# Two projections around a relative attention, each as one written-out block, with one product for both key biases

## The reference, cut to what matters

```python
x = x + rel_attention(layernorm(x), ...)     # q, k, v = h @ W.T + b
#   logits = q k + q rk,  rk[q, k] = embK[clip(k - q, -64, 64) + 64];  w = softmax(logits)
#   out = w v + w rv,     rv from embV in the same way;                out @ Wo.T + bo
x = x + ffn(layernorm(x), ...)
#   h = layernorm(x) * ln1_g + ln1_b;  q, k, v = split(h @ w_qkv + b_qkv);  attention;  @ w_o + b_o
#   then a second layernorm, a top-2 gate over 8 experts, and the experts
```

## Time and profile before

| | us |
|---|---|
| median of 3 runs | 4641.74 |
| lowest and highest | 4637.56, 4656.35 |
| profiled execution | 4656.61 |
| its span in the profile | 4654.9 |
| PE busy | 4083.6 (88%) |
| VectorE busy | 3683.7 (79%) |
| ScalarE busy | 2998.9 (64%) |
| GpSimd busy | 1451.0 (31%) |

### The profile page before, as it was taken

The page is one execution under the profiler, slowest core; times in us unless marked ns, Lnnn a source line. Parts: engine busy times, 40 slices in busy tenths (PEclk is TensorE's granted clock), DMA queues, the critical chain, the costliest instruction groups (busy, mean ns, idle before and its releaser), DMA issues. The chain is left out here.

```text
span 4654.9 us, 79857 instructions
## 1 busy us (share of the span) xinstructions
PE 4083.6 (88%) x26893; PEld 2141.6 (46%) x26893; DVE 3683.7 (79%) x6653; ACT 2998.9 (64%) x5840; POOL 1451.0 (31%) x1418
## 2 busy tenths in 40 slices
PE   2869999999999999997566999999999997769997
PEld 1424444444444444443332333333333332669997
DVE  2678888888888888885467888888888897557775
ACT  0207777777777777775122888888888886246664
POOL 0025666666665656664100000000000000523232
PEclk9959999999999999998785999999999999779999
DMA  2746666666666666665545323323323322676664
GB/s 88 252 99 154 159 164 164 160 166 159 162 168 144 171 148 168 155 165 128 179 162 107 48 40 45 48 40 46 48 39 46 48 39 38 172 213 174 174 178 113
DMA packets 507780, 578.05 MB, mean 124 GB/s; under 512 B 67316, under 2 KB 447268, under 8 KB 497340
## 3 DMA queue, kind: packets, MB, share of 16 engines
q1 hardware_dynamic: 448908, 489.88, 45.1%
q10 hardware_dynamic: 38656, 58.73, 3.4%
q0 software_dynamic: 19824, 24.52, 3.3%
HBM read 365.10 MB, written 210.95 MB: 124 GB/s over the span
## 5 line engine op out<-in xcount | busy, mean ns | idle before, releaser
L633 DVE TENSOR_REDUCE pa_pm<-pa_psA 128x2 f32<-128x1024 f32 x1068 | 1260.2, 1219 | 138.5 <-PE pa_psA L724 138.5
L1234 DVE TENSOR_REDUCE ra_pm<-ra_psA 128x1 f32<-128x896 f32 x1074 | 1167.8, 1087 | 221.7 <-PE ra_psA L1360 210.9
L1327 ACT ACTIVATE ra_p<-ra_psS 128x512 f32<-128x512 f32 x2052 | 1093.3, 605 | 383.4 <-PE ra_psS L1400 272.9
L698 ACT ACTIVATE pa_p<-pa_psS 128x512 f32<-128x512 f32 x2054 | 1066.9, 604 | 247.9 <-PE pa_psS L747 243.4
L724 PE MATMUL pa_psA<-pa_zs,pa_qs 48*128 48x512 f32 x2136 | 829.6, 471 | 50.3 <-DVE pa_recb L664 29.2
L747 PE MATMUL pa_psS<-pa_qs,pa_zs 50*128 50x512 f32 x2056 | 797.4, 464 | 75.8 <-ACT pa_p L698 61.3
L1360 PE MATMUL ra_psA<-ra_zs,ra_qs 48*128 48x512 f32 x2148 | 774.5, 456 | 51.1 <-DVE ra_rst L1253 27.8
L1400 PE MATMUL ra_psS<-ra_qs,ra_zs 50*128 50x512 f32 (+3 forms) x2183 | 718.7, 412 | 29.6 <-ACT ra_p L1327 14.0
L747 PEld LDWEIGHTS pa_psS<-pa_qs,pa_zs 50*128 50x128 f32 x2056 | 343.2, 184 | 620.6 <-ACT pa_p L698 603.1
L1431 PE MATMUL ra_psO<-ra_p,ra_vs 128*32 128x512 f32 (+3 forms) x6400 | 571.6, 463 | 0.0
L758 PE MATMUL pa_psO<-pa_p,pa_vs 128*32 128x512 f32 x4096 | 547.1, 606 | 0.0
(11 more groups left out here) (250 smaller groups left out, 5164.0 us busy)
## 6 DMA issues: line engine op xcount, KB each, us to landing
relative_rows<-ra_rst SPq DMA_DIRECT2D x136, 512.0 KB, 3.9
ra_blk<-window_rows SPq DMA_DIRECT2D x128, 512.0 KB, 4.6
mo_w_raw<-ffn_W SPq DMA_DIRECT2D x58, 1024.0 KB, 5.5
ra_zs<-k_halves SPq DMA_DIRECT2D x204, 248.0 KB, 7.2
ra_dl<-relative_rows SPq DMA_DIRECT2D x136, 256.0 KB, 5.2
window_rows<-ra_pc SPq DMA_DIRECT2D x128, 256.0 KB, 4.5
pa_qs<-q_halves SPq DMA_DIRECT2D x210, 128.0 KB, 6.4
pa_zs<-k_halves SPq DMA_DIRECT2D x210, 128.0 KB, 7.2
```

Source lines behind the costliest of these rows:

```text
L633: dve.reduce_max(pm[:, par, 2 * a:2 * a + 2], psA[w][:, :, :], AX.X).then_inc(s_am.h, 1)
L698: act.activation(pr[:, i % NPR, :], psS[:, slot(i), :], ACT.Exp).then_inc(s_ex.h, 1)
L1234: dve.reduce_max(pm[:, q, i, 2 * left:2 * left + 1], psA[w][:, lo:lo + 2 * G - P], AX.X).then_inc(s_far.h, 1)
L1327: act.activation(dst, psS[:, slot(i), :], ACT.Exp if kind == "E" else ACT.Copy).then_inc(s_cp.h, 1)
```

## The change

The setup and the first projection become one block, `rel_projection`, in which every group is written out instead of looped over. SP loads the first group of x first, then the three weights, then the small vectors; `ev_side` is filled on VectorE from two rows per partition (`ev2`). GpSimd writes identity, zeros and masks. There are four PSUM banks for products; the two key products are each read twice, with the left and the right bias, and the two instructions on VectorE and one on ScalarE for a part become one on each: ScalarE reads PSUM, adds the bias and rounds; VectorE reads PSUM, adds the bias and subtracts the high part. SP issues all stores. The table work of the relative attention is done behind group 0.

The output stage and the second projection become one block, `middle_stage`: output rows of group g + 2 are made inside group g, the residual rows stay in SBUF for the normalisation and are stored from there, and two PSUM banks alternate for products as before. The query scale is multiplied into weight and bias once. `layer_norm` is the old chain of steps as a helper.

In the diff below, `weight` transposes or copies one weight, `root` is the square root, `stationary` copies the transposed rows, `residual` adds the output product to x plus bias, `out_rows` makes that product.

```diff
-                    for step in range(NU + LAG if NU else 0):
-                        if step < NU:
-                            m, n, w = step, NU * g + step, step % 2
-                            _, bias, scale, _ = units[m]
-                            s_u.wait(dve, n + 1)
-                            s_hi.wait(dve, n - 1)
-                            s_lo.wait(dve, n - 1)
-                            dve.tensor_scalar(full[:, w, :], psU[:, w, :], bias, scale, ALU.add, ALU.mult
-                                              ).then_inc(s_full.h, 1)
-                        if 0 <= step - 1 < NU:
-                            m, n, w = step - 1, NU * g + step - 1, (step - 1) % 2
-                            s_hi.wait(dve, n + 1)
-                            dve.tensor_tensor(out=parts[:, slot(q, m), 1, :], in0=full[:, w, :],
-                                              in1=parts[:, slot(q, m), 0, :], op=ALU.subtract).then_inc(s_lo.h, 1)
-                        for _, _ in zip(range(PER), ahead):
...
+def rel_projection(nc, A, ident, sel, masks, e_stack, evc, ev_side, q2, kl2, kr2, v_rows, dr_p):
...
+    NX = 3
+    OUTS = [(0, 0, q2, 0), (1, 1, q2, P), (2, 4, kl2, 0), (2, 6, kr2, 0), (3, 5, kl2, P), (3, 7, kr2, P)]
+    NO, BY_UNIT = len(OUTS), (1, 2, 4, 6)
...
+            sp.dma_start(x[:, 0, :, :], xv[0]).then_inc(s_x[0].h, 16)
+            for i, n in enumerate(("attn_Wq", "attn_Wk", "attn_Wv")):
+                sp.dma_start(raw[:, i, :, :], A[n].rearrange("(a p) c -> p a c", p=P)).then_inc(s_w[i].h, 16)
...
+                for c in range(CH):
+                    sp.dma_start(cols[:, c:c + 1], column(A["attn_bq"], c)).then_inc(s_bias.h, 16)
...
+                sp.dma_start(x[:, 1, :, :], xv[1]).then_inc(s_x[1].h, 16)
+                sp.dma_start(vb[:, :], bcast_rows(A["attn_bv"])).then_inc(s_vb.h, 16)
+                sp.dma_start(x[:, 2, :, :], xv[2]).then_inc(s_x[2].h, 16)
...
+                    row = A["attn_embV"][r:r + 1, :]
+                    sp.dma_start(ev2[:, side, :], bass.AP(row.tensor, row.offset, [[0, P], [1, DK]])
+                                 ).then_inc(s_emb.h, 16)
...
+            for g in range(NG):
+                q = g % 2
+                for o, (_, _, dst, row) in enumerate(OUTS):
+                    s_lo.wait(sp, NO * g + o + 1)
+                    sp.dma_start(dst[:, row:row + P, g * G:(g + 1) * G].rearrange("a p t -> p a t"),
+                                 parts[:, q, o, :, :].bitcast(F32)).then_inc(s_po[q][o].h, 16)
+                    if o == 0 and 3 <= g + 2 < NG:
+                        s_h.wait(sp, TPG * g)
+                        sp.dma_start(x[:, (g + 2) % NX, :, :], xv[g + 2]).then_inc(s_x[(g + 2) % NX].h, 16)
+                s_vo.wait(sp, 2 * g + 2)
+                sp.dma_start(vv[g], vout[:, q, :, :]).then_inc(s_vd[q].h, 16)
+                sp.dma_start(tables[g].rearrange("i q r -> q i r"),
+                             zero[:, :].rearrange("p (i r) -> p i r", r=W)).then_inc(s_zd.h, 16)
...
+                ahead = normalise(dve, g + 1) if g + 1 < NG else iter(())
+                for o, (m, col, _, _) in enumerate(OUTS):
+                    s_hi.wait(dve, NO * g + BY_UNIT[m])
+                    dve.scalar_tensor_tensor(out=parts[:, q, o, 1, :], in0=psU[:, m, :], scalar=cols[:, col:col + 1],
+                                             in1=parts[:, q, o, 0, :], op0=ALU.add, op1=ALU.subtract
+                                             ).then_inc(s_lo.h, 1)
+                    for _ in zip(range((2, 2, 1, 1, 1, 0)[o]), ahead):
...
+            weight(0, psU[:, 2, :])
+            root(0)
+            weight(1, psU[:, 3, :])
+            stationary(0)
+            weight(2, psV[:, 0, :, :].rearrange("p a c -> p (a c)"))
+            for g in range(NG):
+                q = g % 2
+                for o, (m, col, _, _) in enumerate(OUTS):
+                    s_u.wait(act, 4 * g + m + 1)
+                    if g == 0 and o == 0:
+                        s_bias.wait(act, 16 * 6)
+                    if g == 0 and col == 4:
+                        s_col.wait(act, 4)
+                    s_po[q][o].wait(act, 16 * (g // 2))
+                    act.activation(parts[:, q, o, 0, :], psU[:, m, :], ACT.Identity, bias=cols[:, col:col + 1]
+                                   ).then_inc(s_hi.h, 1)
+                    if o == 3 and g + 1 < NG:
+                        root(g + 1)
+                if g + 1 < NG:
+                    stationary(g + 1)
...
+                for m in range(4):
+                    if g == 0 and m % 2 == 0:
+                        s_wc.wait(pe, m // 2 + 1)
+                    if g > 0:
+                        s_lo.wait(pe, NO * (g - 1) + BY_UNIT[m])
+                    for c in range(CH):
+                        last = pe.matmul(psU[:, m, :], wt[:, c, m * P:(m + 1) * P], hT[:, q, c, :],
+                                         start=c == 0, stop=c == CH - 1)
+                    last.then_inc(s_u.h, 1)
...
+def middle_stage(nc, A, ident, ot_rows, x1_rows, f_rows, q2, kl2, v_rows):
...
+    OUTS = [(0, 0, q2, 0), (1, 1, q2, P), (2, 2, kl2, 0), (3, 3, kl2, P)]
...
+                for o, steps in enumerate((5, 2, 5, 0)):
+                    for _ in zip(range(steps), ahead):
+                        pass
+                    s_hi.wait(dve, 4 * g + o + 1)
+                    dve.scalar_tensor_tensor(out=parts[:, q, o, 1, :], in0=psU[:, o % 2, :], scalar=cols[:, o:o + 1],
+                                             in1=parts[:, q, o, 0, :], op0=ALU.add, op1=ALU.subtract
+                                             ).then_inc(s_lo.h, 1)
+                for _ in ahead:
+                    pass
+                if g + 2 < NG:
+                    residual(g + 2)
...
+                    if g + 1 < NG and o in (0, 3):
+                        root(2 * (g + 1) + (o == 3))
+                    if g == 0 and o == 0:
+                        s_scale.wait(act, 2)
+                    s_u.wait(act, 4 * g + o + 1)
+                    s_po[q][o].wait(act, 16 * (g // 2))
+                    act.activation(parts[:, q, o, 0, :], psU[:, o % 2, :], ACT.Identity, bias=cols[:, col:col + 1]
+                                   ).then_inc(s_hi.h, 1)
...
+                for m in range(4):
+                    s_lo.wait(pe, 4 * g + m - 1)
+                    for c in range(CH):
+                        last = pe.matmul(psU[:, m % 2, :], wt[:, c, m * P:(m + 1) * P], hT[:, q, c, :],
+                                         start=c == 0, stop=c == CH - 1)
+                    last.then_inc(s_u.h, 1)
+                if g + 2 < NG:
+                    out_rows(g + 2)
...
-        ident_and_ones(nc, ident)
-        selection(nc, ident, sel)
...
+            rel_projection(nc, A, ident, sel, masks, e_stack, evc, ev_side, q2, kl2, kr2, v_rows, dr_p)
...
+        middle_stage(nc, A, ident, ot_rows, x1, f_rows, q2, kl2, v_rows)
+        plain_attention(nc, ident, sel, q2, kl2, v_rows, den_d, rec_d, ot_rows)
```

858 lines of the change are left out of this document (409 added, 449 removed).

## The result

The changed kernel takes 4460.94 us (median of 4 runs, 4453.53 to 4474.94) against 4639.65 us for the kernel before (4 runs, 4631.86 to 4656.35). The ratio is 0.9614, 95% interval 0.9577 to 0.9651. The profiled executions are 4474.94 and 4656.61 us: 181.7 us apart, where the sum said 182. The changed kernel's four runs differ among themselves by 21 us.

The account below looks back on a forecast made before the run. Bound by a chain of loads and blocks in the setup, then PE and its waits in both projections. Setup and first projection 90.4 us plus middle 92 make 182, off 4641.7: forecast 4460, range 4425 to 4505.

Parts of the forecast that it names:

- the chain that sets the period: First projection: variance, root, last high parts, last low part, normalised rows and transposes in series set a 14.9 us period.
- the late third product: Middle: normalisation steps and root ahead of the first parts delay the third product to 5.1; period 17.8 us.
- Setup: Before the first projection: one block, no 36 us `ev_side` wait; first product at 14.2 instead of 86.56, 72.4 us earlier.
- First projection's period: First projection: one third of PE's products removed and cheaper parts bring a group to 14.9 us from 17.65.
- Cold first group: First projection's group 0: 3.1 us extra over a steady group, plus 1 us for table work.
- Pause behind the first stage: From v's issue to the relative attention: 6.85 us as before, plus 1.9 for zeros and 1.3 for 26 semaphores.
- Middle: Between the attentions: first product at 2216.0, groups of 17.8 us against 21.57; 92 us saved.
- Attentions: Relative and plain attention: same code, so no change in time; wrong if their own time differs by over 20 us.
- transfers: Rival, chance 0.10: transfers through one queue pace the first projection at 18 us a group, losing 22 us: 4482.
- `k_side`: Rival, chance 0.04: in the setup the 36 us wait sat on `k_side`'s 4-byte runs and stays: 4487.
- The clock rival: Rival, chance 0.20: clock falls once a group, 3.1 us each; 25 us per projection stage: 4485 to 4510.
- The attention that stays cold: Rival, chance 0.04: relative attention's clock rises late; over 0.5% slower if its opening clock lasts 410 us longer.

Follow-up runs that it names:

- experiment 8: Changed kernel with both stages reordered, GpSimd's addition in a free slot, and ScalarE's first root ahead of the weight copies; 4435.45 us, ratio 0.9534.
- experiment 10: Kernel of experiment 8 with zero transfers sent one group earlier and semaphores cleared by SyncE, ScalarE and VectorE instead of SyncE alone; ratio 0.9523.
- experiment 6: Kernel of experiment 5 with the middle reordered: first high part before the root, first two low parts back to back; 4445.30 us.
- experiment 5: Changed kernel with the middle's residual rows loaded ahead of stores and GpSimd's addition held until VectorE added the previous group's residual; 4453.88 us.
- the repeat: The changed kernel measured and profiled once more without any edit; 4465.18 us, ratio 0.9602.
- Experiment 2: Changed kernel with each of the two key products computed twice in the first projection; 4480.24 us.
- experiment 3: Changed kernel with the middle's GpSimd addition held until VectorE has taken the group's first reciprocal; 4461.29 us.
- experiment 1: Changed kernel with `ev_side` loaded again as 3840 runs of 64 B in place of the two ev2 loads and VectorE copies; 4484.47 us.

## Why the prediction was right

The forecast was 4460, the median 4460.94. What the change does was read rightly: the wait for `ev_side`, the key product, the chain that sets the period and the late third product are all confirmed by a run. That the total fits to 1 us is luck: the first stage gained 12.3 us too much, the attentions lost 13.2 that stood at nothing, and inside the middle further errors cancelled.

- **Setup**: first product at 12.73, predicted 14.2. x took 3.5 us from issue to the statistics, not 4.6. The root's extra 1.5 us was right in kind and size: the variance was ready at 6.8 and the root ran at 8.2, and moving it won 1.5 us in experiment 8. The cause of the 36 us was named rightly.
- **First projection's period**: 13.65, predicted 14.9. The chain was right, its links too long: high parts take 0.69 alone and 1.25 a pair, where I took 0.75 each. So the third low part starts 0.35 us earlier than predicted, the last two high parts end at 8.9 instead of 9.7 and the rows at 10.9 instead of 11.9; from there to the next group it is 2.7 us instead of 3.0. The two pairs account for some 0.7 of the 1.25 us, TensorE's work behind the rows for 0.3, small steps for the rest. I had said that 0.1 us of error moves the period by some 0.3; 0.12 us a part moved it by 0.7. This is the largest mis-sized term of the stage: 7 x 1.25 = 8.8 us. The low part (0.75, of bounds 0.683 and 1.43) was right.
- **Cold first group**: I charged 3.1 us for it and 1 us for the table work; group 0 took 14.68, 1.0 over the period. Its 16 passes took 7.43 us, 0.4 more than in a steady group. The cold start was not gone, it was nearly over: TensorE had begun with the weights' transposes at 5.16, 7.6 us ahead of the products, where in the kernel before the last transposes began 2.7 us ahead of them (83.83 and 86.56), and the transposes at 10.08 still ran at half speed. This term was 3.1 us too dear.
- **Pause behind the first stage**: 11.5 us from v's issue, predicted 10.05. The transfers ran to 126.4, 5.8 us behind v's issue, since about two of the four key stores (1 MB) were still under way at 120.6; before they had ended 2.6 us behind it, and I had added 1.9. The silence after them grew from 4.3 to 5.7 us, near the 1.3 that I had charged for 26 more semaphores; the price of 0.05 us each stands in no row, and experiment 10 gives some 0.03 (an estimate: 1.0 us for two thirds of 53). (The sum also has a slip: 122.6 and 10.7 and 0.9 make 134.2, not 134.4.) With all this the stage gained 102.7 instead of 90.4.
- **Middle**: 92.1 for 92, by errors that cancel. The order's cost was read rightly (third product late, removed in experiment 6). The collision of GpSimd with VectorE was not read at all and cost 9.4 us; the earlier trace rows have GpSimd's addition with nothing of VectorE beside it. Without it the period is 16.64 us (experiment 5) instead of the 17.8 predicted. Half of this 1.2 us is TensorE's own sum, 14.9 us by experiment 6 (74.6 / 5) where I had 15.5, half the waits of the chain. I also counted seven equal periods, and the last was 15.1 without output rows. In the repeat the same stage took 173.9 us: there GpSimd's additions, which wait for the residual rows, fell otherwise, the third product waited for more than 1.28 us in five groups instead of four, and three pairs of products ran at half clock instead of two.
- **Attentions**: I let them stand at nothing; they cost 20.2 and gave back 7.0 in the profiled pair. The 20.2 of the relative attention alone are just over the 20 us at which I had said I would be wrong. The cause is time at half clock, as above; a term for it is missing in the sum.
- **Rivals**: transfers (13.65 us moved to 12.27 by order alone) and `k_side` fell. The clock rival fell for the first projection; in the middle it came true in two of the groups, at 1.8 us each and not the 3.1 of the earlier trace rows, which is the price of the cold start: 3.6 us of the 25 that it had for this stage. The attention that stays cold fell at its opening, where the rise came 6 us later, not hundreds; a weaker form of it, an attention with more time at half clock, is what this pair shows, and whether the change is its cause is open.

## What to carry to other kernels

Read a stage with four engines as a chain of who waits for whom in one group, and ask of each idle stretch whether it lies ahead of or behind the chain: 3.5 us of products ahead of it cost 2.9, though 2.2 us of idle time stood behind, and one line of order was worth 1.4 us, half as much as the removed product. Before an elementwise step is put on GpSimd, look which of VectorE's steps on SBUF it will run beside, and give it a slot beside PSUM work. A total that fits is no proof of its terms; compare them one by one, those too that stand at nothing: code that is the same before and after can still take another time, and the time that it spent at half clock tells by how much.

## What the runs showed of the hardware

- A GpSimd addition of 2.34 us on SBUF stretched VectorE's small additions of two SBUF tensors from 0.31 to 2.49 us and its SBUF-to-SBUF rows from 1.38 to 3.41, but not statistics (1.39) or additions from PSUM (0.69).
- TensorE kept full clock with 2.24 us of idle time in each 13.65 us. In the middle the length of one gap did not decide it: behind gaps of 3.45 and 3.38 us two products took 5.4 us instead of 3.6, and behind 2.72 us one took its 1.99. Experiment 2 has the same middle, but there a gap of 3.24 us left the clock alone and one of 2.59 us was followed by the slow pair (its PE timeline below; 1.98 us is for one product, 5.40 for two). In experiment 3 a product behind gaps of 1.28 and 2.21 us, with one of 1.98 us between them, took 3.3 to 3.7 us.

```profile
2193.90 1.98 PE L1766 MATMUL mid_psU<-mid_hT,mid_w_qkv 128*128 128x512 f32 x4 [3.24 <-DVE mid_parts L1677]
...
2231.73 5.40 PE L1766 MATMUL mid_psU<-mid_hT,mid_w_qkv 128*128 128x512 f32 x8 [2.59 <-DVE mid_parts L1677]
```

- The same relative attention took 1947.5 to 1976.8 us in twelve profiles, 0.43 us more for each us that it spent at half clock (240.9 to 307.7 us).
- 64-byte runs moved at 7 GB/s again (experiment 1). The two `ev_side` loads, of 120 KB each and one behind the other, landed 22.1 and 37.2 us after their issue.
- Behind the last transfer of a stage 4.3 to 5.7 us (first stage) and 3.2 to 4.5 us (middle) pass before the next stage's first work; in the tenth kernel, where three engines clear the semaphores instead of one, it was 1.0 and 1.3 us less than in the eighth.
